# An attention and mixture kernel: output bias as one bf16 pass over three-part factors, a transpose in another PSUM bank, and zeros multiplied before the first data

## The chip, the cores and the metric

The kernel runs on one core of a Trainium2 chip. The metric is the device time of one execution in microseconds (us), the median of several runs. The core has five engines that run their own instruction streams and wait for each other on semaphores: PE (TensorE, matrix multiply), DVE (VectorE), ACT (ScalarE), POOL (GpSimd) and SP (SyncE, which here only issues DMA transfers). PE writes to PSUM, eight banks of 128 partitions by 512 f32.

## What is computed

Input `x` is 8 sequences of 512 rows of 256 numbers. A first layer adds an attention-like gate and normalizes; a second adds a mixture of 12 experts and normalizes again. Cut to what matters here:

```python
x  = layernorm(x + attn(x))                # sum of exp(scores) per row, a small gate, fc2
xa = x @ P_w.T                             # C1, C2, C3: [rows, 12], softmax over the top 3, zero elsewhere
h  = gelu(sum_e C1[:, e:e+1] * (x @ W1[e].T))
y  = sum_e C2[:, e:e+1] * (h @ W2[e].T) + C3 @ b2      # C3 @ b2 is the output bias
x  = layernorm(x + y)
```

## The kernel before, in words

The 4096 rows are 32 tiles of 128 rows (`NT`), in 8 groups of 4 (`GT`, `NG`). The program has two stages.

**The early stage** goes over 8 chunks `c` of attention work: `project(c, 0..3)` on PE (f32, weights `wqk`, input `xTb` from DMA), `qk_copy` on ACT (PSUM bank to SBUF), `rope` on DVE, `scores` on PE, `exps` on ACT, `gate_transpose` on PE. PE, ACT and DVE each begin it with a wait for `ld_const`, six transfers of constants; PE waits for `ld_qk` (`wqk`) too. Beside that the expert weights arrive (`ld_w[0]`, `ld_w[1]`, two transfers of 1 MB and 2 MB each). DVE finds the largest of the first (`w_amax`), ACT sums the second (`w_sum(0)` after chunk 1), and from both come the scales. Then each weight is split into two f16 parts: 8 by ACT and DVE (`w_high`, `w_low`), 16 by POOL (`w_piece`, three instructions each). The group work of the first tiles is placed between chunks by `early_aux`.

**The main stage** is a loop over `i`. In iteration `i`, PE does the second mixture of tile `i-2` (three experts, 18 matmuls with `hT`), transposes the gelu output of tile `i-1` (L916), and does the first mixture of tile `i` (18 matmuls with `x1T`). DVE adds each product with its weight out of PSUM (L1202; of the first mixture ACT takes the first product, L599), ACT does gelu (L604) and the final scaling (L657), POOL the power of the variance (L457 to L459). Products lie in four PSUM banks in turn, so a product waits until the one four places before it has been added. Once in a group of four iterations, with `s = i % 4`, the functions `aux(k, s, pos)` of every engine put in the routing of the next group; `pos` 0 stands ahead of the second mixture, `pos` 1 between the L916 transposes and the first mixture. Order on each engine is the order written in the code.

What the change touches there: at (3, 1) POOL makes the weights of the next group (`weights_of`: L406, L408 for the third weights `C3`, L409 for the others) and then selects those of the chosen experts (`select_of`, six copies at L421). At (0, 0) PE turns `C3`, padded to 32 columns a tile, with one f32 transpose of 128x128 (`C3_transpose`, L772) into `bank[MISC]`, and ACT copies it to `C3T` (L561). At (0, 1) PE computes the router's logits (L755), the gate's `fc` (L732) and, where a group begins, loads the experts' numbers (`load_ids`, L847). At (1, 1) and (2, 1) PE does `bias(g, h)` (L784): one f32 matmul of K = 64 over 512 columns for two tiles; DVE adds it (L1110).

The banks `MISC` (logits, counts, `C3T`), `XPOSE` (the transposes of `x1`, L741, read by ACT's `x1_high` L555 and DVE's `x1_low` L1049) and `ROWS` (`fc` and `bias`) are shared.

## Time and profile before

| | |
|---|---|
| Median of 3 runs | 322.95 us (322.84 to 324.55) |
| Profiled execution, its own time | 323.53 us |
| Its span (first to last instruction) | 321.8 us |
| Granted TensorE clock, mean | 0.981 |
| Busy: PE, DVE, ACT, POOL | 88%, 78%, 48%, 36% |
| Largest groups on PE | L832 mixtures 152.4 us, L688 projections 64.3 us |
| L784 bias matmuls | 32 records, 18.0 us |

How to read it: engines run side by side, so busy shares do not add up, and a group's busy time is not what it costs the kernel. What an edit is worth is read from which wait ends last at its place. Matmul records overlap (their ends are modelled), so the time from one start to the next is the measure of what PE spends. A matmul in f32 leaves two records.

### The profile page before, as it was taken

The page shows a single profiled execution, that of the slowest core. Times are in us where ns is not written, and L with a number is a line of the kernel's source. Part 1 is how long each engine was busy: PE and PEld are TensorE (multiplying, and loading weights), DVE is VectorE, ACT ScalarE, POOL GpSimd, SP SyncE. Part 2 cuts the span into 40 slices and gives each one's busy share as a digit, 9 for nine tenths or more (in the row PEclk, how much of TensorE's full clock was granted, in tenths as well). Part 3 has the DMA queues.
Part 4 walks back from the last instruction along what each step waited for, and adds up shares of the span by engine and source line. Part 5 has one row for each costly group of instructions (what it writes and reads, how often), then busy time and mean ns, then how long its engine had stood idle before and what let it go on. Part 6 is the DMA issues. An engine that isn't in the chain of part 4 may idle for free.

```text
span 321.8 us, 6235 instructions
## 1 busy us (share of the span) xinstructions
PE 282.4 (88%) x1976; PEld 191.8 (60%) x1978; DVE 250.2 (78%) x744; ACT 155.8 (48%) x327; POOL 115.0 (36%) x264
## 2 busy tenths in 40 slices
PE   0999999979784989999999999999999997989981
PEld 0444455444333668677677667677678576667770
DVE  0169789999976579689789879888978977887672
ACT  1138747657561381435635634633733753724331
POOL 1000028999999102142332331522333324132221
PEclk9999999999985999999999999999999999999998
DMA  8999999900000000000010001000100010011011
GB/s 232 415 404 229 200 151 211 144 3 0 0 1 0 3 2 0 18 18 18 18 33 17 18 18 29 22 18 18 34 20 16 18 34 19 18 33 26 26 35 37
DMA packets 19235, 20.58 MB, mean 64 GB/s; under 512 B 1600, under 2 KB 18432, under 8 KB 18688
## 3 DMA queue, kind: packets, MB, share of 16 engines
q1 hardware_dynamic: 18480, 19.22, 24.8%
q10 hardware_dynamic: 720, 0.93, 1.0%
q8 instruction: 18, 0.29, 0.4%
q14 instruction: 17, 0.14, 0.1%
HBM read 15.94 MB, written 4.19 MB: 63 GB/s over the span
## 4 chain that ended last, share of the span: by engine, by line
DVE 25%; PE 21%; issue 6%; ACT 5%; POOL 3%; DVEq 0%; POOLq 0%
PE bank L832 17%; DVE early L1202 11%; DVE st L1239 3%; DVE stats L1038 2%; DVE top L1059 2%; ACT x L548 2%; DVE early L1244 2%; PE bank L784 2%; ACT early L657 1%; POOL rstd L391 1%; PE bank L741 1%; DVE mv L1240 1%; ACT x1T L555 1%; ACT early L604 1%; DVE esum L1104 1%
## 5 line engine op out<-in xcount | busy, mean ns | idle before, releaser
L832 PE MATMUL bank<-W,early 128*128 (+1 forms) x630 | 75.5, 273 | 4.4 <-DVE early L1244 2.3
L832 PE MATMUL bank<-W,x1T 128*128 (+1 forms) x630 | 76.9, 277 | 0.5 <-DVE early L1202 0.3
L832 PEld LDWEIGHTS bank<-W,x1T 128*128 128x128 f16 x630 | 60.3, 99 | 19.8 <-DVE early L1202 9.5
L688 PE MATMUL bank<-early,wqk 128*128 128x512 f32 x128 | 64.3, 634 | 8.5 <-DMA gatew<-in_gate 8.5
L1202 DVE SCALAR_TENSOR_TENSOR early<-bank,Csel,early 128x256 f32<-128x256 f32 x124 | 59.3, 479 | 15.0 <-PE bank L832 10.5
L832 PEld LDWEIGHTS bank<-W,early 128*128 128x128 f16 x630 | 60.1, 98 | 14.8 <-DVE early L1244 3.3
L457 POOL TENSOR_SCALAR ve<-mv 128x1 f32<-128x1 f32 x32 | 7.3, 230 | 117.2 <-DVE mv L1240 117.2
L688 PEld LDWEIGHTS bank<-early,wqk 128*128 128x128 f32 x128 | 23.5, 201 | 30.1 <-issue 20.9
L604 ACT ACTIVATE early<-early 128x256 f32<-128x256 f32 x32 | 13.3, 417 | 48.0 <-DVE early L1202 47.9
L499 ACT ACTIVATE qk<-bank 128x512 bf16<-128x512 f32 x32 | 19.0, 594 | 35.6 <-PE bank L688 35.4
L599 ACT ACTIVATE early<-bank,Csel 128x256 f32<-128x256 f32 x31 | 14.6, 472 | 31.0 <-PE bank L832 30.7
L965 DVE TENSOR_TENSOR xcos<-qk,cb 128x1024 bf16<-128x1024 bf16 x16 | 11.8, 740 | 20.0 <-ACT qk L499 20.0
L390 POOL TENSOR_SCALAR ve<-mv 128x4 f32<-128x4 f32 x8 | 2.3, 283 | 65.1 <-DVE mv L1042 65.0
L647 ACT ACTIVATE early<-bank,ipow 128x256 f16<-128x256 f32 x32 | 15.0, 467 | 16.5 <-PE bank L916 16.5
L382 POOL TENSOR_TENSOR W<-wtmp,W 128x512 f16<-128x512 f32 x16 | 21.1, 1317 | 1.4
L657 ACT ACTIVATE early<-early,shift,rstd 128x256 f32<-128x256 f32 x32 | 18.8, 586 | 5.1 <-POOL shift L459 5.1
L1049 DVE TENSOR_TENSOR x1T<-bank,x1T 128x512 f16<-128x512 f32 x16 | 11.0, 688 | 12.3 <-ACT x1T L555 12.3
L548 ACT ACTIVATE x<-xs,shift,rstd 128x256 f32<-128x256 f32 x32 | 17.4, 591 | 4.3 <-POOL shift L393 4.3
L458 POOL TENSOR_TENSOR rstd<-ve,minus_half 128x1 f32<-128x1 f32 x32 | 18.0, 563 | 2.7
L509 ACT ACTIVATE expd<-bank 128x128 bf16<-128x128 f32 (+3 forms) x32 | 13.7, 435 | 10.0 <-PE bank L703 9.9
L732 PE MATMUL bank<-fc2s,hgT 32*128 32x256 f32 x64 | 18.0, 400 | 0.0
L784 PE MATMUL bank<-b2s,C3T 64*128 64x512 f32 x32 | 18.0, 641 | 0.0
(107 smaller groups left out, 422.3 us busy)
## 6 DMA issues: line engine op xcount, KB each, us to landing
early<-in_xT SPq DMA_DIRECT2D x16, 256.0 KB, 9.8
xs<-in_x SPq DMA_DIRECT2D x32, 128.0 KB, 7.3
out<-early SPq DMA_DIRECT2D x32, 128.0 KB
W<-in_w1T SPq DMA_DIRECT2D x1, 2048.0 KB, 12.0
W<-in_w2T SPq DMA_DIRECT2D x1, 2048.0 KB, 12.3
W<-in_w1T SPq DMA_DIRECT2D x1, 1024.0 KB, 7.6
W<-in_w2T SPq DMA_DIRECT2D x1, 1024.0 KB, 13.8
wqk<-in_wqkT ACTq DMA_DIRECT2D x1, 512.0 KB, 3.8
```

What stands on the lines that cost most here:

```text
L382: pool.tensor_tensor(W[:, m, e + 1, 1, :], wtmp[:, n % 2, :], W[:, m, e + 1, 0, :], ALU.subtract)\
L458: link(pool.tensor_tensor(rstd2[:, p:p + 1], ve2[:, p:p + 1], minus_half[:, 0:1], ALU.pow))
L499: act.activation(qk[:, c % 2, g, :, :].rearrange("p s n -> p (s n)"), bank[PROJ[n % 2]][:, :], ACT.Copy)\
L548: n = act.activation(x1[:, g % 3, t, :], xs[:, GT * g + t, :], ACT.Identity, bias=shift[:, g % 2, t:t + 1], scale=rstd[:, g % 2, t:t + 1])
L604: act.activation(hact[:, t % 2, :], acc1[:, t % 2, :], ACT.Gelu).then_inc(gelu_done, 1)
L647: act.activation(hT[:, t % 2, 0, :, :].rearrange("p c n -> p (c n)"), bank[HT][:, 0:DIM], ACT.Copy, scale=ipow2[:, 1:2]).then_inc(hhi_done, 1)
L657: act.activation(y[:, t % 4, :], y[:, t % 4, :], ACT.Identity, bias=shift2[:, p:p + 1], scale=rstd2[:, p:p + 1]).then_inc(y_done, 1)
L688: mm = pe.matmul(bank[PROJ[n % 2]][:, :], wqk[:, k, g, :], xTb[:, c % 4, k, :, :].rearrange("p s n -> p (s n)"), start=(k == 0), stop=(k = ...
L732: mm = pe.matmul(bank[ROWS][:, t % 2 * DIM:(t % 2 + 1) * DIM], hgT[PAD * T:PAD * (T + 1), u, :, :].rearrange("p b r -> p (b r)"), fc2s[PAD ...
L784: mm = pe.matmul(bank[ROWS][:, :], C3T[rows, :], b2s[rows, :], start=True, stop=True)
L832: mm = pe.matmul(where[:, 0:DIM], lhs(hx, c), w, start=(k == 0), stop=(k == 5))
L1202: dve.scalar_tensor_tensor(sums, bank[place[n]][:, 0:DIM], c, before, ALU.mult, ALU.add)\
```

## The change

1. **The bias in bf16.** `b2` and `C3` are each written as a sum of three bf16 parts. Six products of parts (indices `LEFT` and `RIGHT`) are stacked along K, 6 x 12 = 72 rows, so that one bf16 matmul per tile of K = 72 and 256 columns gives the bias. POOL splits `b2` once at the start (12 partitions, four instructions); SP then spreads the parts to 72 partitions with six transfers in SBUF, in place of four loads from memory.
2. **`C3` is split on POOL** in each group by a new function `C3_split`, four instructions behind `select_of`. `weights_of` now writes `C3f`, and its last instruction waits for that one.
3. **`C3_transpose`** is four bf16 transposes (72 x 128 each) into `bank[XPOSE]` and moves on PE from (0, 0) to (0, 1), ahead of the logits. It no longer waits for `ids_done`; it waits for `x1lo_done`. ACT's `C3T_copy`, now of 72 x 512, moves to (0, 1); in the first group it stands behind `gate_relu(NCH - 1)`.
4. **At the start** PE multiplies zeros (28 matmuls of 256 columns) before it waits for `ld_qk`, and the waits for `ld_const` on PE and ACT move behind the first projections and copies.

```diff
+        WARM = 28
             load_chunk(1)
+            sp.dma_start(b2f[:, :], b2e[1:NS, :]).then_inc(ld_b2, 16)
             load_experts(0, w1T)
...
-            sp.wait_ge(zero_done, 1)
-            for t in range(GT):
-                rows = slice(PAD * t, PAD * (t + 1))
-                sp.dma_start(b2s[rows, t % 2 * DIM:(t % 2 + 1) * DIM], b2e[rows, :]).then_inc(ld_rows, 16)
+            sp.wait_ge(b2_split, 1)
+            for k in range(NP):
+                sp.dma_start(b2s[NE * k:NE * (k + 1), :], b2p[:, RIGHT[k], :]).then_inc(b2_spread, 16)
...
+            pool.wait_ge(ld_b2, 16)
+            link(pool.tensor_copy(b2p[:, 0, :], b2f[:, :]))
+            link(pool.tensor_tensor(b2f[:, :], b2f[:, :], b2p[:, 0, :], ALU.subtract))
+            link(pool.tensor_copy(b2p[:, 1, :], b2f[:, :]))
+            pool.tensor_tensor(b2p[:, 2, :], b2f[:, :], b2p[:, 1, :], ALU.subtract).then_inc(b2_split, 1)
...
             def weights_of(g):
                 pool.wait_ge(recip_done, g + 1)
-                wait(pool, C3T_done, g)
...
-                pool.tensor_tensor(C3[:, :, 1:NS], w[:, :, NM, :], s[:, :, NM, :], ALU.mult).then_inc(C3_done, 1)
+                link(pool.tensor_tensor(C3f[:, :, :], w[:, :, NM, :], s[:, :, NM, :], ALU.mult))
...
+            def C3_split(g):
+                wait(pool, C3T_done, g)
+                f = C3f[:, :, :].unsqueeze(2)
+                link(pool.tensor_copy(C3[:, :, 0:3, :], f.to_broadcast([P, GT, 3, NE])))
+                link(pool.tensor_tensor(C3f[:, :, :], C3f[:, :, :], C3[:, :, 0, :], ALU.subtract))
+                link(pool.tensor_copy(C3[:, :, 3:5, :], f.to_broadcast([P, GT, 2, NE])))
+                pool.tensor_tensor(C3[:, :, 5, :], C3f[:, :, :], C3[:, :, 3, :], ALU.subtract).then_inc(C3_done, 1)
...
                     weights_of(k + 1)
                     select_of(k + 1)
+                    C3_split(k + 1)
...
             def C3_transpose(g):
                 pe.wait_ge(C3_done, g + 1)
-                pe.wait_ge(ids_done, g + 1)
-                pe.transpose(bank[MISC][:, 0:P], C3[:, :, :].rearrange("p t n -> p (t n)"), identf[:, :])\
-                    .then_inc(C3T_done, 1)
+                wait(pe, C3T_copied, g)
+                pe.wait_ge(x1lo_done, min(2 * (g + 2), 2 * NG))
+                spread = bank[XPOSE][0:NP * NE, 0:GT * P // 2].bitcast(BF16)
+                for t in range(GT):
+                    tr = pe.transpose(spread[:, t * P:(t + 1) * P], C3[:, t, :, :].rearrange("p k e -> p (k e)"),
+                                      const(C_IDENT, P))
+                tr.then_inc(C3T_done, 1)
...
-                mm = pe.matmul(bank[ROWS][:, :], C3T[rows, :], b2s[rows, :], start=True, stop=True)
+                if g == 0 and h == 0:
+                    pe.wait_ge(b2_spread, 16 * NP)
+                for t in (2 * h, 2 * h + 1):
+                    mm = pe.matmul(bank[ROWS][:, t % 2 * DIM:(t % 2 + 1) * DIM], C3T[:, t, :], b2s[:, :], start=True, stop=True)
...
             def aux(k, s, pos):
-                if (s, pos) == (0, 0) and group(k):
-                    C3_transpose(k)
                 if (s, pos) == (0, 1):
+                    if group(k):
+                        C3_transpose(k)
                     if group(k + 1):
                         route_logits(k + 1)
...
-            pe.wait_ge(ld_const, 16 * 6)
+            pe.wait_ge(zero_done, 1)
+            for n in range(WARM):
+                pe.matmul(bank[SCORE[n % 2]][:, 0:DIM], zeros[:, 0:P], zeros[:, :], start=True, stop=True)
             pe.wait_ge(ld_qk, 16)
```

How it moves instructions, at the two places of the main loop that matter. First PE, where a group begins (iteration `i = 4k`), before. The names are output `<-` inputs; `C` is the third weights' tile, `early` holds `hT` and the gelu output, and what a row waits for stands in brackets:

```order
L832 MATMUL bank<-W,x1T 128x256 x5
L772 MATMUL bank<-identf,C 128x128 [waits ids_done,C3_done]
L832 MATMUL bank<-W,early 128x256 [waits slot_added,hlo_done]
L832 MATMUL bank<-W,early 128x256 x5
...
L916 MATMUL bank<-identf,early 128x128 [waits hlo_done,gelu_done]
L916 MATMUL bank<-identf,early 128x128
L755 MATMUL bank<-MT,x1T 128x36 [waits C3T_copied,MT_done,x1lo_done]
L755 MATMUL bank<-MT,x1T 128x36 x23
L732 MATMUL bank<-fc2s,hgT 128x256 [waits fc_added]
L732 MATMUL bank<-fc2s,hgT 128x256
L847 TENSOR_LOAD ids [waits ids_done]
```

The same place on PE in the changed kernel, from the L916 transposes on (its lines have other numbers):

```order
L953 MATMUL bank<-identf,early 128x128
L802 MATMUL bank<-cb,C 72x128 [waits x1lo_done,C3T_copied,C3_done]
L802 MATMUL bank<-cb,C 72x128 x3
L782 MATMUL bank<-MT,x1T 128x36 [waits ids_done,MT_done,x1lo_done]
L782 MATMUL bank<-MT,x1T 128x36 x23
L758 MATMUL bank<-fc2s,hgT 128x256 [waits fc_added]
L758 MATMUL bank<-fc2s,hgT 128x256
L880 TENSOR_LOAD ids [waits ids_done]
```

The transpose of the third weights now stands behind the second mixture and the L916 transposes, with its wait for `C3_done`, and ahead of the logits, of `fc` and of the load of the experts' numbers.

Next POOL at the end of a group (`i = 4k + 3`), before:

```order
L459 TENSOR_SCALAR shift<-mv,rstd 128x1 [waits pool_step]
L406 TENSOR_TENSOR escale<-esum,cscale 128x12 [waits C3T_done,recip_done]
L408 TENSOR_TENSOR C<-ez,escale 128x4x12 [waits pool_step]
L409 TENSOR_TENSOR C<-ez,escale 128x8x12
L415 TENSOR_LOAD ids [waits C_done,ids_done]
L421 ISA
L421 COPY Csel<-C 128x4
...
L457 TENSOR_SCALAR ve<-mv 128x1 [waits y_done,mv2_done]
```

And in the changed kernel:

```order
L421 TENSOR_TENSOR escale<-esum,cscale 128x12 [waits recip_done]
L423 TENSOR_TENSOR C3f<-ez,escale 128x48 [waits pool_step]
L424 TENSOR_TENSOR C<-ez,escale 128x8x12 [waits pool_step]
L438 TENSOR_LOAD ids [waits C_done,ids_done]
L444 ISA
L444 COPY Csel<-C 128x4
...
L430 CAST C<-C3f 128x4x36 [waits C3T_done]
L431 TENSOR_TENSOR C3f<-C3f,C 128x48 [waits pool_step]
L432 CAST C<-C3f 128x4x24 [waits pool_step]
L433 TENSOR_TENSOR C<-C3f,C 128x4x12 [waits pool_step]
L482 TENSOR_SCALAR ve<-mv 128x1 [waits y_done,mv2_done]
```

What PE's transpose waits for was L408, the second instruction of `weights_of`. It is now L433, the last of `C3_split`, behind the load, the six copies and three instructions linked one to the next.

## Rows read from the trace of the kernel before

**Rows 1.** Windows, five groups of the main stage, 133.08 to 260.97 us: sums and means
```profile
sum 127.89, PE 120.97 PEld 90.65 DVE 109.77 ACT 65.93 POOL 39.80; mean PE 24.19 PEld 18.13 DVE 21.95 ACT 13.19 POOL 7.96
```

**Rows 2.** Timeline of PE in a group: start, length, line, operation, idle before and releaser
```profile
213.69 2.14 PE L832 MATMUL bank<-W,x1T 128*128 x18
216.13 0.33 PE L772 MATMUL bank<-identf,C 128*128 128x128 f32 x1 [0.30 <-POOL C L408]
...
218.62 0.77 PE L755 MATMUL bank<-MT,x1T 128*128 128x36 f16 x24
...
220.38 2.14 PE L832 MATMUL bank<-W,x1T 128*128 x18
...
224.64 1.12 PE L784 MATMUL bank<-b2s,C3T 64*128 64x512 f32 x2
...
229.47 0.84 PE L832 MATMUL bank<-W,early 128*128 x6 [0.33 <-DVE early L1202]
...
232.15 0.66 PE L741 MATMUL bank<-identf,x 128*128 128x128 f32 x4 [0.31 <-ACT x L548]
```

**Rows 3.** Timeline of DVE in the same group
```profile
215.94 0.48 DVE L1202 SCALAR_TENSOR_TENSOR early<-bank,Csel,early 128x256 f32<-128x256 f32 x1 [0.17 <-PE bank L832]
...
217.88 0.69 DVE L1049 TENSOR_TENSOR x1T<-bank,x1T 128x512 f16<-128x512 f32 x1 [0.86 <-ACT x1T L555]
...
222.77 1.00 DVE L1202 SCALAR_TENSOR_TENSOR early<-bank,Csel,early 128x256 f32<-128x256 f32 x2
```

**Rows 4.** Timeline of POOL in the same group
```profile
216.03 0.35 POOL L409 TENSOR_TENSOR C<-ez,escale 128x96 f32<-128x96 f32 x1
217.21 0.82 POOL L421 COPY Csel<-C 128x4 f32 x6 [0.83 <-POOL C L409]
220.77 0.23 POOL L457 TENSOR_SCALAR ve<-mv 128x1 f32<-128x1 f32 x1 [2.73 <-DVE mv L1240]
221.08 0.56 POOL L458 TENSOR_TENSOR rstd<-ve,minus_half 128x1 f32<-128x1 f32 x1
```

**Rows 5.** Groups by line and form, POOL, five groups of the main stage: busy us, mean ns
```profile
L421 POOL COPY Csel<-C 128x4 f32 x30 | 4.2, 193 | 4.3 <-POOL C L409 4.1 <-issue 0.2
L398 POOL TENSOR_TENSOR ez<-ez,mask 128x144 f32<-128x144 f32 x5 | 2.3, 458 | 0.0
```

**Rows 6.** One line each: duration in ns, shortest, median, longest
```profile
L966 DVE TENSOR_TENSOR xsin<-qk,cb x16: 679/685/1648, 15.6 to 96.6; 128x1024 bf16<-128x1024 bf16 x16
...
L847 PEldq TENSOR_LOAD <-ids x8: 592/680/783, 114.9 to 290.4; - x8
```

**Rows 7.** Timeline of the start, PE, SP and ACT
```profile
8.53 5.71 PE L688 MATMUL bank<-early,wqk 128*128 128x512 f32 x8 [8.53 <-DMA gatew<-in_gate]
...
13.86 0.43 SPq L314 DMA_DIRECT2D W<-in_w2T  x1
...
14.73 7.13 PE L688 MATMUL bank<-early,wqk 128*128 128x512 f32 x16
...
27.27 1.89 ACT L516 ACTIVATE junk<-W 128x2048 bf16<-128x2048 f32 x1
```

**Rows 8.** DMA issues: size, us from issue to landing
```profile
W<-in_w2T SPq DMA_DIRECT2D x1, 2048.0 KB, 12.3
```

**Rows 9.** Timeline at the end of the early stage, PE, and DVE behind it
```profile
101.03 0.45 PE L772 MATMUL bank<-identf,C 128*128 128x128 f32 x1 [5.94 <-DVE ids L1099]
101.27 4.63 PE L832 MATMUL bank<-W,x1T 128*128 128x256 f16 x24
...
118.66 1.01 DVE L1202 SCALAR_TENSOR_TENSOR early<-bank,Csel,early 128x256 f32<-128x256 f32 x2 [1.22 <-ACT early L599]
```

**Rows 10.** The chain that ended last, the last two groups: start, us, what
```profile
275.72 1.05 PE bank L784 x2
276.77 4.04 PE bank L832 x36
...
289.77 0.33 PE bank L772
```

More of the change, by code:

```diff
@@ L35 @@
 WS = NE + 2
+LEFT, RIGHT = (0, 0, 0, 1, 1, 2), (0, 1, 2, 0, 1, 0)
+NP = len(LEFT)
 EPS = 1e-5
@@ L105, in build @@
         fc2s = sb("fc2s", [P, DIM], F32)
-        b2s = sb("b2s", [P, 2 * DIM], F32)
+        zeros = sb("zeros", [P, DIM], BF16)
+        b2f = sb("b2f", [NE, DIM], F32)
+        b2p = sb("b2p", [NE, 3, DIM], BF16)
+        b2s = sb("b2s", [NP * NE, DIM], BF16)
         iota12 = sb("iota12", [P, NE], F32)
@@ L133, in build @@
         Csel = sb("Csel", [P, NT, NM, TOPK], F32)
-        C3 = sb("C3", [P, GT, PAD], F32)
-        C3T = sb("C3T", [P, P], F32)
+        C3f = sb("C3f", [P, GT, NE], F32)
+        C3 = sb("C3", [P, GT, NP, NE], BF16)
+        C3T = sb("C3T", [NP * NE, GT, P], BF16)
         used = sb("used", [1, NM, NE], F32)
@@ L172, in build @@
         ld_rows = sem("ld_rows")
+        ld_b2 = sem("ld_b2")
+        b2_split = sem("b2_split")
+        b2_spread = sem("b2_spread")
         ld_seq = [sem(f"ld_seq{i}") for i in range(4)]
@@ L367, in link @@
                 pool.wait_ge(pool_step, steps[0])
-            pool.memset(b2s[:, :], 0.0).then_inc(zero_done, 1)
+            pool.memset(zeros[:, :], 0.0).then_inc(zero_done, 1)
             pool.memset(ones3[:, :], 1.0).then_inc(zero_done, 1)
             pool.memset(minus_half[:, :], -0.5).then_inc(zero_done, 1)
-            pool.memset(C3[:, :, :], 0.0).then_inc(zero_done, 1)
-            pool.wait_ge(zero_done, 4)
+            pool.wait_ge(zero_done, 3)
+            pool.wait_ge(ld_b2, 16)
[3 more added lines that the diff above has]
+            pool.tensor_tensor(b2p[:, 2, :], b2f[:, :], b2p[:, 1, :], ALU.subtract).then_inc(b2_split, 1)
             def w_piece(n):
@@ L448, in _ @@
             select_of(0)
+            C3_split(0)
             for i in range(NT + 2):
@@ L560, in C3T_copy @@
                 wait(act, bias_done, 2 * g)
-                act.activation(C3T[:, :], bank[MISC][:, 0:P], ACT.Copy).then_inc(C3T_copied, 1)
+                act.activation(C3T[:, :, :].rearrange("p t n -> p (t n)"),
+                               bank[XPOSE][0:NP * NE, 0:GT * P // 2].bitcast(BF16), ACT.Copy).then_inc(C3T_copied, 1)
             def early(k, s, pos):
@@ L576, in aux @@
             def aux(k, s, pos):
-                if (s, pos) == (0, 0):
-                    if group(k + 1):
-                        x1_high(k + 1, 1)
-                    if group(k):
-                        C3T_copy(k)
+                if (s, pos) == (0, 0) and group(k + 1):
+                    x1_high(k + 1, 1)
+                if (s, pos) == (0, 1) and group(k):
+                    C3T_copy(k)
                 if (s, pos) == (1, 0) and group(k + 1):
@@ L604, in gelu @@
                 act.activation(hact[:, t % 2, :], acc1[:, t % 2, :], ACT.Gelu).then_inc(gelu_done, 1)
-            act.wait_ge(ld_const, 16 * 6)
             for c in range(NCH):
@@ L609, in _ @@
                 qk_copy(c, 1)
+                if c == 0:
+                    act.wait_ge(ld_const, 16 * 6)
                 if c:
@@ L631, in _ @@
             aux(0, 0, 0)
-            aux(0, 0, 1)
             begin(0)
@@ L636, in _ @@
             gate_relu(NCH - 1)
+            aux(0, 0, 1)
             gelu(0)
@@ L724, in fc @@
                 if g == 0 and h == 0:
-                    pe.wait_ge(ld_rows, 16 * 5)
+                    pe.wait_ge(ld_rows, 16)
                 if h == 0:
@@ L738, in x1_transpose @@
                 wait(pe, x1lo_done, 2 * g + h)
+                wait(pe, C3T_copied, g - 1)
                 for t in range(2):
@@ L749, in route_logits @@
                     pe.wait_ge(scale_done, 1)
-                wait(pe, C3T_copied, g)
+                wait(pe, ids_done, g)
                 for t in range(GT):
@@ L782, in bias @@
                     wait(pe, bias_added, 2 * g + 1)
-                rows = slice(2 * PAD * h, 2 * PAD * (h + 1))
-                mm = pe.matmul(bank[ROWS][:, :], C3T[rows, :], b2s[rows, :], start=True, stop=True)
+                if g == 0 and h == 0:
+                    pe.wait_ge(b2_spread, 16 * NP)
+                for t in (2 * h, 2 * h + 1):
+                    mm = pe.matmul(bank[ROWS][:, t % 2 * DIM:(t % 2 + 1) * DIM], C3T[:, t, :], b2s[:, :], start=True, stop=True)
                 mm.then_inc(bias_done, 1)
@@ L858, in _ @@
                 if c == 0:
+                    pe.wait_ge(ld_const, 16 * 6)
                     for k in range(NC):
```

## Prediction

> **What bounds the kernel now.** I read the windows of the main stage first, to see whether one engine is full. None is: five middle groups take 127.89 us, 25.58 each, and of that PE is busy 24.19 and DVE 21.95 [rows 1]. What an edit does in one of them counts five times. Then I read the timelines of that group engine by engine, looking only for the idle time ahead of an instruction and for who ended it. PE waits 0.30 us for POOL's third weights, 0.33 for a DVE addition that frees a product bank, and 0.31 for ACT's normalized `x` [rows 2]. DVE waits 0.17 for a product and 0.86 for ACT's copy of `x1T` [rows 3], and the additions at 222.77 wait for nothing. So PE and DVE take turns: PE is the fuller, but after each of its cheap places something else lets it go on. The reader should take from this that PE's time is worth something only where no wait stands behind it. Last I read the chain that ended last. In the two last groups it does run through PE, the bias matmuls included [rows 10]: there no normalization of a coming group is left and PE's time is the kernel's.
>
> **Shorter bias matmuls.** A pass took 1.05 us; 36 matmuls of 256 columns took 4.04, 0.112 each, so two take 0.22 and a pass saves 0.83 [rows 10]. There are 16.
> - In the five middle groups the pass at 224.64 is followed by the wait for DVE at 229.47, the group's second pass by the wait for ACT at 232.15 [rows 2]. Both waits end by work that DVE set in motion, so they grow by what PE saves. I cost the ten passes at nothing; the cover is DVE's own work from 217.88 on. Without that cover they would be worth 8.3 us.
> - Of the first group's two, the first has DVE waiting 1.22 us for ACT beside it [rows 9], so it is hidden; for the second the timeline has no wait close behind, and I count it: -0.8 (bounds 0 and -1.7).
> - The last two groups' four are on the chain: -3.3.
>
> **The transpose of the third weights.** Leaving (0, 0) takes PE's wait of 0.30 and the transpose away at 216.13. It gains nothing by itself: the next product additions start only after DVE's L1049, which waits for ACT [rows 3]. At (0, 1) it waits for the end of `C3_split`. POOL's six copies end at 217.21 + 0.82 = 218.03 [rows 4]; the new link in `weights_of` moves them by 0.1. The four instructions of the split are not in the trace. Two are subtractions of 48 elements; 0.35 for 96 elements and 0.46 for 144 [rows 4, 5] put 48 at 0.25 to 0.28. Two are casts of 144 and 96 elements, between 0.19 (a copy of four elements) and 0.46 (144 elements with two inputs) [rows 5]; with one input I take 0.30 each, nearer the copy. Three links cost 0.08 each (221.00 to 221.08) [rows 4]. Sum 1.4 us, bounds 1.0 (four at 0.19) and 1.7. So PE is released at about 219.55.
>
> The four bf16 transposes: four f32 ones took 0.66 [rows 2], and 4 x 128 columns at the pace above take 0.22. I take 0.25, bounds 0.22 and 0.66. The logits then start at 219.8 where they started at 218.62, 1.2 us late, and so does the first mixture, 220.38 to 221.6 (`fc` and the load of the ids, 0.68 [rows 6], lie between and overlap as before). How much of it DVE feels: in the iteration before, DVE added the third product 2.25 us after the mixture's start (213.69 to 215.94), having waited for it [rows 2, 3]. From 220.38 that is 222.63, but DVE reached it only at 223.27, the second of the two from 222.77 [rows 3]. The slack is 0.64, and 1.2 - 0.64 = 0.56 us is new delay on DVE. All later waits of the group hang on DVE, so the group grows by it: 5 x 0.56 = +2.8. Each 0.1 us of the split, or of the transposes, is 0.5 us here. Behind the waiting transpose stand the logits, `fc`, the ids and the first mixture; who waits for them is DVE (`route_max`, which it reaches well after, so hidden) and DVE and ACT for the products.
>
> In the last two groups PE is the path. Before, PE was released at 289.77 [rows 10] and had about 2.35 us of work up to the first mixture: 18 matmuls at 0.112 and the two L916 transposes. Now it is released 3.4 us after that point, does its transposes (0.25), and in the last group the load of the ids, until now hidden, shows with 0.68 [rows 6], as no `fc` or logits cover it. That is 1.1 us in the one group and 2.1 in the other: +3.2. With the four bias passes the end is -0.1.
>
> ACT's `C3T_copy` grows from 128 to 512 columns; DVE takes 0.69 for 512 [rows 3], I take 0.5 for ACT. In the middle groups it falls into ACT's idle time. In the first it now stands ahead of `gelu(0)`, where DVE waits for ACT [rows 9]: +0.5 (bounds 0.3 and 0.7).
>
> **A rule that speaks against it.** Beside POOL, DVE's L966 has taken up to 1.65 us where the median is 0.69 [rows 6]; but the addition at 215.94 took 0.48 while POOL ran L409 at 216.03 [rows 3, 4], so I add nothing for the additions that will run beside the split. The Trainium skill (Advanced Engine Details and Errata, VectorE Performance Modes) says that VectorE's second port is shared with GpSimd and that the two block each other in the two-port modes. By the rule a DVE instruction in such a mode beside the split would grow as L966 did, by up to 0.96 us a group, 4.8 in five; by the row it is zero, and the row decides.
>
> **The start.** PE's eight first records took 5.71 us, sixteen later ones 7.13, 0.446 each [rows 7]: 2.1 us went to a pace half as fast, the lower of the clock's two levels (1.2 and 2.4 GHz). Zeros multiplied before should take it away, and PE starts before 8.53, as soon as `wqk` and chunk 0 are there. But ACT comes to `w_sum(0)` at 27.27, and that needs the last 2 MB of the second weights, issued at 13.86 and landed 12.3 later, at 26.2 [rows 7, 8]. DMA is full throughout, so this does not come earlier: only 1.1 us of the gain passes, and DVE's scales, POOL's sixteen pieces and all behind them move by that. -1.1 (bounds 0 and -1.3). SP's six small transfers in place of four, and POOL's split of `b2`, are over long before anything needs them.
>
> At the end of the early stage PE stood 5.94 us for `ids_done` and then did four products in 4.63, 0.193 a matmul against the 0.112 of the end, so mostly at the lower clock [rows 9, 10]. Now three of the four can run before; the fourth waits for DVE, which has to finish the ids, `fc_add` and `x1_low` (0.7 each) first. That is worth about 1.7 us at the fourth product. But PE then resumes at the same time as before, with its clock just as low, and the scores and the next products pay for it. I take -0.9 (bounds 0 and -2).
>
> **The sum.** -1.1 - 0.9 + 0.5 - 0.8 + 2.8 - 0.1 = +0.4 against a span of 321.8 us; with 1.7 around it, as in the profiled execution (323.53), 323.9, and against the median of 322.95, **323.3**. From here on I count from the median.
>
> **The rivals.**
> - *The split is slower, or the transposes are* (the other side). Place: PE at (k, 0, 1). Price: with 1.7 for the split and 0.5 for the transposes 0.55 us more in each of seven groups, 327; half of that, 325.3. It decides (past +1.6 us) when split and transposes together exceed 1.9 us where I have 1.65. For it: POOL's casts with a broadcast operand are in no row, and the links may be dearer in four-dimensional forms. Against: no POOL row of this size is over 0.46.
> - *The split is quick and the clock stays up at 101 us.* Split 1.0: -0.4 in each of seven groups, -2.8; 320.5, and with the clock up to 1 us less. For it: copies at 0.19 [rows 5]. Against: 144 elements are not four.
> - *PE is the bound after all.* If DVE had room, a middle group would change by PE's own sum, +1.2 - 1.7 = -0.5, so -2.3 in place of +2.8: 318.2. For it: 24.19 of 25.58 us busy [rows 1]. Against: the two waits behind the two passes [rows 2].
>
> **How the numbers follow.** About 0.5% (1.6 us) is what a measurement of this kernel tells from no change. Forecast, gain and loss about even (321.4 to 324.5): 0.42. Slower split: 0.30. Quick split: 0.20. PE bound: 0.08. So faster 0.28, same 0.42, slower 0.30. The bounds of all terms added up reach from 319 to 329; leaving out PE bound and the last of the slow side, the range is 320.2 to 326.5.
>
> **What would show it.** In the profile after: L714 at 0.43 a record from its first; ACT's `w_sum(0)` at 26.2; the four instructions of `C3_split` with a sum of 1.4 us; PE idle ahead of L802 by about 1 us each group, ended by POOL; the waits behind the two bias passes grown to about 1 us each; a middle group of 26.1 us instead of 25.58; the end shorter by 0.1. Wrong it would be if POOL finished the split before PE arrives at it, if DVE's slack of 0.64 were larger because its own order moved, or if the low clock at 101 us came otherwise.

## The result, and the profile after

The changed kernel takes 335.07 us (median of 4 runs, 334.39 to 335.85) where the kernel before takes 323.13 (4 runs, 322.84 to 324.55): a ratio of 1.036, 95% interval 1.032 to 1.040. It is slower by 12 us. The profiled execution took 334.84 us with a span of 333.1, 11.3 more than before. The times of single executions hang on the granted clock of TensorE, so below I give that clock where they spread.

Page of the changed kernel, the busy times and the clock row (40 slices of the span, tenths of the full clock):

```profile
PE 284.6 (85%) x2028; PEld 201.0 (60%) x2030; DVE 250.0 (75%) x744; ACT 159.0 (48%) x327; POOL 125.0 (38%) x299
...
PEclk9999999999796979979979996999899979997997
```

And the clock row of the page before:

```profile
PEclk9999999999985999999999999999999999999998
```

This is the whole result at a glance. Before, the clock fell twice at the end of the early stage (from 87.6 and from 97.8 us) and never in the main stage but for its last 2 us. After, it falls in those two places again, and then once in nearly every group. The windows of the changed kernel, from the HT transposes of the first group's third tile to the same instruction five groups on, and then each group from one transpose of the third weights to the next (columns: window and length, busy time of each engine with its count, granted clock, DMA share, GB/s):

```profile
133.84:273.20 139.36, 121.74 (x1023) 95.42 (x1021) 110.15 (x386) 68.17 (x130) 45.01 (x150) 0.93 0.07 20
...
142.05:169.67 27.62, 24.05 (x205) 18.81 (x205) 22.03 (x78) 13.61 (x26) 9.00 (x30) 0.94 0.07 21
169.67:197.31 27.64, 24.00 (x205) 18.70 (x205) 22.05 (x78) 13.62 (x26) 9.00 (x30) 0.94 0.07 21
197.31:226.16 28.85, 25.64 (x205) 19.80 (x205) 21.97 (x77) 13.72 (x26) 8.99 (x30) 0.88 0.07 19
```

Five groups took 127.89 before [rows 1] and take 139.36 now. The work of PE became less (the bias passes), yet PE's busy time did not fall with it (121.74 us, before 120.97). One group closer, around the transposes:

```profile
167.70:171.20 3.50, 2.00 (x36) 1.66 (x34) 3.03 (x8) 1.36 (x3) 1.92 (x11) 1.00 0.13 37
171.20:174.60 3.40, 3.40 (x15) 2.02 (x14) 1.66 (x15) 0.47 (x1) 0.82 (x2) 0.50 0.00 0
174.60:198.50 23.90, 20.25 (x191) 16.41 (x189) 20.05 (x62) 13.14 (x25) 7.95 (x27) 1.00 0.09 24
198.50:205.30 6.80, 6.80 (x29) 4.45 (x29) 3.61 (x22) 1.09 (x3) 1.05 (x3) 0.50 0.00 0
```

PE is busy only 2.00 us of the first 3.50, and then works through the next 3.40 at 0.50, the lower level (1.2 GHz). The timeline of PE there, which answers to [rows 2]:

```profile
167.78 0.38 PE L953 MATMUL bank<-identf,early 128*128 128x128 f32 x2
169.67 0.41 PE L802 MATMUL bank<-cb,C 128*72 128x128 bf16 x4 [1.50 <-POOL C L433]
169.92 0.76 PE L782 MATMUL bank<-MT,x1T 128*128 128x36 f16 x24
170.61 1.54 PE L758 MATMUL bank<-fc2s,hgT 32*128 32x256 f32 x4
172.08 3.35 PE L865 MATMUL bank<-W,x1T 128*128 x18
...
181.74 0.84 PE L865 MATMUL bank<-W,early 128*128 x6 [0.60 <-DVE early L1239]
...
182.88 0.38 PE L817 MATMUL bank<-b2s,C3T 72*128 72x256 bf16 x2
184.40 0.66 PE L768 MATMUL bank<-identf,x 128*128 128x128 f32 x4 [1.14 <-ACT x L573]
```

The reader should see three things. PE stands 1.50 us for the end of the split (L433). Right behind it, the mixture that took 2.14 takes 3.35 with the same 18 matmuls. And the waits behind the two shorter bias passes have grown, from 0.33 and 0.31 to 0.60 and 1.14. POOL's split in that group, which answers to [rows 4]:

```profile
168.27 0.30 POOL L430 CAST C<-C3f 128x144 bf16<-128x144 f32 x1
168.65 0.28 POOL L431 TENSOR_TENSOR C3f<-C3f,C 128x48 f32<-128x48 f32 x1
168.99 0.26 POOL L432 CAST C<-C3f 128x96 bf16<-128x96 f32 x1
169.34 0.28 POOL L433 TENSOR_TENSOR C<-C3f,C 128x48 bf16<-128x48 f32 x1
```

168.27 to 169.62 is 1.35 us, where I had 1.4. So the wait itself was foreseen, but not what the clock does behind it. In windows of the granted clock I count eight such dips of about 3.4 us from 119 us to 310 us (one of twice that length counts as two). There is one behind each of the stalls at 142.05, 169.67 and 302.83, two behind 197.31, one behind the 1.14 us waits at 239.26 and 266.93 each, and one behind a wait of 2.25 at 119.21. Waits of the same length also pass with the clock up:

```profile
226.16 0.41 PE L802 MATMUL bank<-cb,C 128*72 128x128 bf16 x4 [1.50 <-POOL C L433]
...
281.40 0.41 PE L802 MATMUL bank<-cb,C 128*72 128x128 bf16 x4 [2.25 <-POOL C L433]
```

So does the stall at 253.83, and so do the waits for `normed` at 156.77, 184.40 and 213.26. A wait of this length can bring a dip; it does not bring one each time.

### The profile page after: what moved, and what is told of

The parts are those of the page before. It is cut to its first block, busy times and chain, and to the rows that moved or that the text cites. A ratio compares the mean times of both kernels' runs of the same rounds, so it can differ in the third digit from the quotient of the medians.

```text
span 333.1 us, 6370 instructions
## 1 busy us (share of the span) xinstructions
PE 284.6 (85%) x2028; PEld 201.0 (60%) x2030; DVE 250.0 (75%) x744; ACT 159.0 (48%) x327; POOL 125.0 (38%) x299
## 4 chain that ended last, share of the span: by engine, by line
PE 36%; POOL 20%; DVE 19%; issue 8%; ACT 6%; SPq 4%; DMA 4%; POOLq 2%; DVEq 0%
PE bank L865 25%; DVE early L1239 7%; POOL W L398 5%; DMA W<-in_w2T 4%; POOL wtmp L395 4%; POOL W L397 3%; PE bank L758 2%; PE bank L714 2%; SPq L325 2%; POOL rstd L407 2%; DVE st L1276 2%; DVE stats L1075 2%; ACT x L573 2%; POOL Csel L444 2%; PE bank L768 1%
## 5 line engine op out<-in xcount | busy, mean ns | idle before, releaser
L865 PE MATMUL bank<-W,x1T 128*128 (+1 forms) x630 | 85.2, 295 | 5.7 <-DVE early L1239 4.1
L865 PE MATMUL bank<-W,early 128*128 (+1 forms) x630 | 78.4, 279 | 6.3 <-DVE early L1281 3.7
L1239 DVE SCALAR_TENSOR_TENSOR early<-bank,Csel,early 128x256 f32<-128x256 f32 x124 | 59.4, 479 | 26.9 <-PE bank L865 21.3
L865 PEld LDWEIGHTS bank<-W,x1T 128*128 128x128 f16 x630 | 64.8, 105 | 23.5 <-DVE early L1239 6.5
L865 PEld LDWEIGHTS bank<-W,early 128*128 128x128 f16 x630 | 61.4, 100 | 18.3 <-issue 4.4
L714 PE MATMUL bank<-early,wqk 128*128 128x512 f32 x128 | 61.7, 613 | 3.5 <-DMA early<-in_xT 1.9
L714 PEld LDWEIGHTS bank<-early,wqk 128*128 128x128 f32 x128 | 22.8, 195 | 24.5 <-issue 22.2
L758 PE MATMUL bank<-fc2s,hgT 32*128 32x256 f32 x64 | 19.3, 422 | 0.0
L768 PE MATMUL bank<-identf,x 128*128 128x128 f32 x64 | 10.9, 296 | 7.9 <-ACT x L573 5.7
```

The source lines that it names most:

```text
L714: mm = pe.matmul(bank[PROJ[n % 2]][:, :], wqk[:, k, g, :], xTb[:, c % 4, k, :, :].rearrange("p s n -> p (s n)"), start=(k == 0), stop=(k = ...
L758: mm = pe.matmul(bank[ROWS][:, t % 2 * DIM:(t % 2 + 1) * DIM], hgT[PAD * T:PAD * (T + 1), u, :, :].rearrange("p b r -> p (b r)"), fc2s[PAD ...
L768: tr = pe.transpose(bank[XPOSE][:, t * DIM + c * P:t * DIM + (c + 1) * P], x1[:, g % 3, 2 * h + t, c * P:(c + 1) * P], identf[:, :])
L865: mm = pe.matmul(where[:, 0:DIM], lhs(hx, c), w, start=(k == 0), stop=(k == 5))
L1239: dve.scalar_tensor_tensor(sums, bank[place[n]][:, 0:DIM], c, before, ALU.mult, ALU.add)\
```

## The experiments

Ratios are to the kernel before, run beside each version (medians 323.96 to 324.04 us).

**Is the idle PE the cause?** PE's idle time ahead of the transposes is filled with work that makes nothing ready sooner.

```diff
             def C3_transpose(g):
-                pe.wait_ge(C3_done, g + 1)
                 wait(pe, C3T_copied, g)
                 pe.wait_ge(x1lo_done, min(2 * (g + 2), 2 * NG))
+                for n in range(12):
+                    pe.matmul(bank[XPOSE][:, 0:DIM], zeros[:, 0:P], zeros[:, :], start=True, stop=True)
+                pe.wait_ge(C3_done, g + 1)
```

> The changed kernel, with 12 matmuls of zeros (256 columns, 1.35 us at 0.112 each) put on PE ahead of its wait for the split third weights, into the bank that the transposes then overwrite. POOL's split and every wait stay as long as they are; PE only does not stand idle in it. Theory A (the idle time of about 1.5 us at this place brings PE's clock down once a group, and that is most of the missing time): the dips of the granted clock in the main stage go away, each of about 3.4 us at half pace worth 1.7 us, seven of them, so 324 to 327 us. Theory B (the clock is not the cause; the delay of the split and of the longer chain through DVE is): 335, since nothing becomes ready sooner. Theory C (the clock falls because the bias passes are shorter, and PE then idles for DVE and ACT behind them): dips stay at about half of the places, 329 to 333.

Measured: 329.42 us (329.32 to 330.0, 4 runs), ratio to before 1.019 (1.015 to 1.022), mean clock 0.974 where the changed kernel had 0.936. Windows by group:

```profile
168.71:195.19 26.48, 23.65 (x219) 19.27 (x217) 22.13 (x77) 13.60 (x26) 9.00 (x30) 1.00 0.08 22
195.19:223.33 28.14, 25.30 (x219) 20.18 (x217) 22.13 (x77) 13.60 (x26) 8.99 (x30) 0.94 0.07 20
```

More work on PE made the kernel 5.6 us faster, so theory B fell. The time lies in theory C's range and above theory A's. The two dips left in the middle groups stand behind ACT's `normed` (L768, 1.14 us). A group with one dip is 28.14 - 26.48 = 1.66 us longer than one without, which is the price of a dip. That it is not 324 to 327 is the edit's own fault. The zeros start only behind the wait for `x1lo_done`, 0.70 us into the stall, and end half a microsecond after the split:

```profile
167.40 1.47 PE L800 MATMUL bank<-zeros 128*128 128x256 bf16 x12 [0.70 <-DVE x1T L1088]
168.71 0.39 PE L804 MATMUL bank<-cb,C 128*72 128x128 bf16 x4
```

**The stall avoided.** The transposes stand behind `route_logits` and `fc` in (0, 1).

```diff
                 if (s, pos) == (0, 1):
-                    if group(k):
-                        C3_transpose(k)
                     if group(k + 1):
                         route_logits(k + 1)
                     if group(k + 2):
                         fc(k + 2, 1)
+                    if group(k):
+                        C3_transpose(k)
```

> The changed kernel, with the transposes of the third weights moved on PE behind the logits and fc of (0, 1), which are 1.9 us of work; the split is then done before PE comes to it, and PE has no stall there. Theory A (the stall of 1.5 us lowers the clock): no dips, and the delay of 1.2 us ahead of the first mixture is gone too: 321 to 324 us. Theory B (only the delay counts, about 0.56 a group and 3.2 in the last two): 335 less 6, 329. Theory C (the waits behind the short bias passes lower the clock): dips stay, behind the waits for ACT's normalized x; 326 to 331.

Measured: 330.89 us median of 8 runs, 325.18 (clock 0.961) to 333.42 (0.937). Its four shortest, up to 330.01, give a ratio of 1.012 (1.007 to 1.017). The only trace is of the longest, 333.42:

```profile
172.02:199.21 27.19, 24.20 (x205) 18.98 (x204) 21.94 (x78) 13.61 (x26) 9.04 (x30) 0.94 0.08 21
...
180.00:183.80 3.80, 2.04 (x16) 1.07 (x14) 3.62 (x15) 2.08 (x6) 1.68 (x4) 1.00 0.02 4
183.80:187.20 3.40, 3.40 (x16) 2.65 (x17) 1.38 (x6) 1.75 (x4) 1.48 (x4) 0.50 0.13 37
```

The stall is gone in the middle groups, and still there is one dip in each of the five, now behind the wait for `normed` (PE busy 2.04 of the 3.80 us ahead of it). Theory A as I put it, that the stall alone does it, is refuted. Theory C holds for this kernel: the dips stand where it says, and its range of 326 to 331 holds the median, though not the executions at 325 and at 333.

**The split cut to one cast.** The second and third parts are left out, so the bias is not the right one.

```diff
             def C3_split(g):
                 wait(pool, C3T_done, g)
                 f = C3f[:, :, :].unsqueeze(2)
-                link(pool.tensor_copy(C3[:, :, 0:3, :], f.to_broadcast([P, GT, 3, NE])))
...
+                pool.tensor_copy(C3[:, :, :, :], f.to_broadcast([P, GT, NP, NE])).then_inc(C3_done, 1)
```

> The changed kernel, but the split of the third weights is a single cast into all six places (the second and third parts are left out, so the bias is not the sum of its parts); the other three instructions and their three links, about 1.1 us, are gone, the order of everything stays. PE's stall should shrink from 1.5 to about 0.5 us. Theory A: dips gone, 322 to 325 us. Theory B: 335 less 0.56 in each of five groups and about 2 at the end, 330. Theory C: dips stay, 328 to 332.

Measured: 324.3 us median of 5 runs, from 320.29 (clock 0.975) to 329.54 (0.944); the three shortest give a ratio of 0.994 (0.987 to 1.000). The windows of the execution of 325.23:

```profile
142.64:168.16 25.52, 22.50 (x204) 18.03 (x205) 21.94 (x78) 13.60 (x26) 8.31 (x27) 1.00 0.08 22
...
193.85:220.71 26.86, 24.02 (x204) 18.99 (x205) 21.88 (x78) 13.60 (x26) 8.30 (x27) 0.94 0.07 20
```

In four of the five middle groups PE's wait at the transposes is 0.70 us now and ends by DVE's L1083, not by the split. In the fifth (193.85) it is 0.86, ended by the cast, and the one dip of the middle groups stands behind that. A group without a dip takes 25.52, 0.06 less than before the change. The waits of 0.60 and 1.14 us behind the bias passes are in all five groups too, and here no dip stands behind them. Between the executions of this one program lie 9 us; their clocks, 0.944 to 0.975, say that the number of dips differs, but only one of them has a trace. Theory A's range holds the median, and no theory foresaw that spread.

**The start alone**, in the kernel before: part 4 of the change and nothing else.

```diff
+            pool.memset(zeros[:, :], 0.0).then_inc(zeros_done, 1)
...
-            pe.wait_ge(ld_const, 16 * 6)
+            pe.wait_ge(zeros_done, 1)
+            for n in range(WARM):
+                pe.matmul(bank[SCORE[n % 2]][:, 0:DIM], zeros[:, 0:P], zeros[:, :], start=True, stop=True)
             pe.wait_ge(ld_qk, 16)
```

> The kernel before, with only part 4 of the change: 28 matmuls of zeros ahead of the wait for wqk, and the waits for the constants behind the first projections and copies. By my prediction this is worth 1.1 us, capped by the landing of the second weights, which ACT's sum waits for: 321.9 us. Rival: the gain of the head is lost in a wait at the end of the early stage, 323; or the later arrival of the x rows in the changed kernel (1 to 4 us later) is due to this part, and it costs time: 324.

Measured: 324.84 us median of 10 runs against 324.04 of 18, ratio 1.001 (0.998 to 1.004). Three executions took 322.6 at a clock of 0.980, seven 324.6 to 325.8 at 0.971 to 0.976. One of the seven, on PE:

```profile
6.99 3.60 PE L693 MATMUL bank<-early,wqk 128*128 128x512 f32 x8
...
29.48 0.70 PE L693 MATMUL bank<-early,wqk 128*128 128x512 f32 x1 [2.84 <-ACT qk L503]
```

The first projections take 3.60 in place of 5.71 [rows 7], as meant. At 29.48 PE then stands 2.84 us for ACT, which waits for the second weights, and the next 3.4 us run at the lower clock. The cap that I had predicted is there, and in this execution it costs: a dip follows the idle time that it makes. 321.9 was expected; the rivals' 323 and 324 are nearer. In the changed kernel PE waits only 1.58 us at this place (28.92), with no dip behind it.

**Which of the two idle times?** The changed kernel with the stall left as it is, and zeros behind the second bias pass.

```diff
             def x1_transpose(g, h):
-                pe.wait_ge(x1_done, 2 * g + h + 1)
                 wait(pe, x1lo_done, 2 * g + h)
                 wait(pe, C3T_copied, g - 1)
+                if g >= 2 and h == 0:
+                    for n in range(8):
+                        pe.matmul(bank[XPOSE][:, 0:DIM], zeros[:, 0:P], zeros[:, :], start=True, stop=True)
+                pe.wait_ge(x1_done, 2 * g + h + 1)
```

> The changed kernel, with 8 matmuls of zeros (256 columns, 0.9 us) on PE behind the second bias pass of a group, where PE otherwise stands 1.14 us for ACT's normalized x. The stall ahead of the split third weights stays. It asks which of two idle times brings the granted clock down. Theory A (the stall ahead of the transposes of the third weights does): dips stay behind that stall once a group, 333 to 335 us. Theory C (the longer wait behind the short bias passes does): dips gone, 326 to 328. Theory D (both places are enough by themselves, whichever of them comes first): dips only behind the stall of the transposes, some fewer than before, 331 to 334.

Measured: 331.11 us (330.18 to 333.68, 4 runs), mean clock 0.950. Windows by group:

```profile
142.25:168.26 26.01, 23.27 (x212) 18.82 (x212) 22.03 (x78) 13.60 (x26) 9.01 (x30) 1.00 0.08 22
168.26:197.12 28.86, 26.57 (x212) 20.45 (x213) 21.98 (x78) 13.74 (x26) 9.00 (x30) 0.88 0.07 20
197.12:223.12 26.00, 23.27 (x213) 18.89 (x213) 22.04 (x78) 13.60 (x26) 9.00 (x30) 1.00 0.08 22
```

The dips that are left stand right behind the stall of 1.5 us, in every other group, twice as long. So theory D is right. With the late transposes only the other wait was left, and here only the stall: each place can bring dips by itself. This run also gives the group with the stall and without a dip: 26.0 us, against 26.1 predicted.

**Both covered**: the late transposes and the 8 zeros together.

> The changed kernel with both idle times taken away: the transposes of the third weights behind the logits and fc, and 8 matmuls of zeros behind the second bias pass. The version with only the first of the two had groups of 27.2 us with one dip each, 25.5 without it. Theories A, C and D all expect the clock up through the middle groups now, groups of 25.5 us, and 324 less up to 2: 321 to 325 us. Theory B, that the clock is only a sign and not the cause, expects 330 as with the transposes moved alone, since zeros make nothing ready sooner.

Measured: 325.26 us median; nine executions lie between 323.14 (clock 0.981) and 325.57 (0.966); ratio 1.003 (1.000 to 1.005), just above the 321 to 325 expected. A tenth execution took 1551.62 us. It is left out of the comparison, and what happened in it stays open. Windows:

```profile
145.03:170.54 25.51, 23.43 (x213) 18.89 (x212) 21.95 (x78) 13.60 (x26) 9.01 (x30) 1.00 0.08 22
170.54:196.05 25.51, 23.43 (x213) 18.75 (x212) 21.95 (x78) 13.60 (x26) 8.99 (x30) 1.00 0.08 22
```

No dip is left in the middle groups, and each takes 25.51. PE multiplies more than in the trace with only the late transposes, and a group is 1.7 us shorter, so theory B is refuted here too. Two dips that the kernel before does not have are left in this trace, one at 120 us and one behind the last group's stall.

**Cheap bias passes alone**, in the kernel before: `C3T` and `b2` in bf16 and one part, nothing moved.

```diff
-        C3T = sb("C3T", [P, P], F32)
+        C3T = sb("C3T", [P, P], BF16)
+        b2h = sb("b2h", [P, 2 * DIM], BF16)
...
-                mm = pe.matmul(bank[ROWS][:, :], C3T[rows, :], b2s[rows, :], start=True, stop=True)
+                mm = pe.matmul(bank[ROWS][:, :], C3T[rows, :], b2h[rows, :], start=True, stop=True)
```

> The kernel before with one edit: the copies of the third weights and of b2 are bf16, one part only (the two lower parts are left out, so the bias has bf16's precision), so that each bias pass is one bf16 matmul of 512 columns, about 0.22 us in place of 1.05. Nothing else moves: no split, no stall. By my prediction's cost of the passes alone: nothing in the middle groups, -0.8 in the first, -3.3 in the last two, 319 us. Theory C (PE's longer waits behind short passes bring the clock down): one dip in most groups, 1.65 each, 322 to 328. Theory A (only the stall of the split does it): 319 to 320, no dips.

Measured: 319.96, 320.11, 327.28 and 327.57 us, at clocks of 0.980, 0.980, 0.961 and 0.966. An execution of the first kind was the profiled one:

```profile
154.29 0.66 PE L745 MATMUL bank<-identf,x 128*128 128x128 f32 x4 [1.04 <-ACT x L552]
...
163.85:189.41 25.56, 22.91 (x199) 17.66 (x200) 21.94 (x78) 13.17 (x26) 7.89 (x27) 1.00 0.08 22
```

The wait grows from 0.31 to 1.04 and takes up what PE saves, so a group stays at 25.56, as I had costed it. With the clock up the whole is worth 4.0 us against the 323.99 of the kernel before beside it (4.1 by the prediction's terms). The other two executions are 3.4 us slower than before. The likely reason is the same dips, as their lower clock says, but neither of them has a trace. So it was tested the other way round, by 7 matmuls of zeros ahead of that wait:

> The kernel before with one-part bf16 bias passes (bf16's precision), and 7 matmuls of zeros (0.8 us) ahead of PE's wait for ACT's normalized x behind the second pass of a group: PE is as busy there as with the f32 passes. The version without the zeros ran 320.0 us in two executions at a mean granted clock of 0.980 and 327.4 in two at 0.961 and 0.966. Theory C (the wait of 1.04 us there tips the clock in some executions): all executions now at about 320 us and 0.98. Rival (the first pass of a group, with its own wait, or another place does it): executions of 323 to 327 us stay.

Measured: 321.66 us (320.76 to 321.95, 4 runs), clock 0.976 to 0.986, ratio 0.993 (0.990 to 0.995). The executions at 327 are gone. With four executions of each, chance is not excluded. Of the 1.6 us against the 320.0 the traces show the place and not the cause: a middle group takes 25.50 (140.16 to 165.66), but the first of them begins at 140.16 in place of 138.26.

**The last group.** Its stall is 2.25 us, and PE sets the end there. Its transposes and ACT's copy move to (1, 0), on top of both covers.

```diff
                 if (s, pos) == (0, 1):
...
-                    if group(k):
+                    if group(k) and k < NG - 1:
                         C3_transpose(k)
+                if (s, pos) == (1, 0) and k == NG - 1:
+                    C3_transpose(k)
```

> As the version with the late transposes and the zeros behind the second bias pass, and in the last group the transposes (and ACT's copy of them) move one iteration on, to (1, 0), where the split is long done. The last group's stall is 2.26 us there, and PE sets the end. Expected by all theories: 1.5 to 2.3 us less than that version, 319 to 323 us, if the last group is bound by PE as the chain shows; nothing, if its end is set by another engine.

Measured: 321.18 us (320.82 to 321.71, 4 runs), ratio 0.991 (0.988 to 0.994). It is the first version with the whole computation that beats the kernel before. It is 4.1 us less than without the edit, where 1.5 to 2.3 were expected: that price left out the dip behind the stall, and 2.25 with 1.65 for the dip would be 3.9. One dip is left in the group before the last, at 271.6 us behind a wait of 1.26 for DVE, and the two next versions have it too.

**The dip at 118 us.** On top of that, 20 matmuls of zeros ahead of the very first bias pass (inside `bias`, where `g == 0 and h == 0`).

> The version with late transposes, zeros behind the second bias pass and the last group's transposes at (1, 0), and 20 more matmuls of zeros (2.2 us) ahead of the very first bias pass, where PE stood 2.83 us for DVE and 6.8 us at the lower clock followed. Theory (any idle time of PE of about a microsecond or more can bring the clock down, and covering it with zeros prevents that): the dip at 118 us goes, 72 products of the second mixture take 8.1 us in place of 10.6, and 1.6 to 3.3 us are won: 318 to 320 us. Rival: DVE sets the time there, and the products only wait less fast: 321, no change. Rival: the clock falls there because of the longer wait at 92 to 101 us, and zeros at 117 come too late: dips stay.

Measured: 320.08 us (318.73 to 321.64, 4 runs), ratio 0.988 (0.983 to 0.992). The windows of the version without these zeros and of this one:

```profile
118.10:124.90 6.80, 5.32 (x26) 3.77 (x27) 5.36 (x19) 3.09 (x5) 1.67 (x4) 0.50 0.00 0
```

```profile
118.00:125.00 7.00, 6.05 (x55) 4.94 (x53) 5.46 (x20) 3.79 (x7) 1.67 (x4) 1.00 0.00 0
```

In about the same stretch PE has 55 instructions in place of 26. The dip there is gone, and with it most of PE's wait (0.64 us in place of 2.83). The median moved by 1.1 us, less than the 1.6 to 3.3 expected, and the runs of the two versions overlap.

**The zeros at the start taken away again** (`WARM = 0`), all else as in the last version.

> The same kernel, but without the 28 matmuls of zeros at the very start (the waits for the constants stay behind the first projections). PE then begins at about 7.6 us at the lower clock, and loses 1.6 us until it rises. By my prediction the head's gain is capped at 1.1 us by the landing of the second weights: 1 us slower than with them. Rival: the gain is lost whole in PE's wait for ACT at about 28 us, and the dip that follows it costs the rest: no slower than with them, or up to 1.6 us faster.

Measured: 320.0 us (319.62 to 320.54, 4 runs), ratio 0.988 (0.986 to 0.990), the same as with them. PE starts at 7.47 at the lower clock and is through the first eight projection records at 12.84, where the changed kernel was at 11.23. But it does not wait at 28 us for ACT any more:

```profile
7.47 5.43 PE L716 MATMUL bank<-early,wqk 128*128 128x512 f32 x8 [7.47 <-DMA early<-in_xT]
...
28.79 1.99 PE L716 MATMUL bank<-early,wqk 128*128 128x512 f32 x4
```

The 28 matmuls at the start are worth nothing in this kernel that these runs can tell; the rival is right.

## Why the prediction was wrong

I forecast 323.3 us (320.2 to 326.5) and 335.07 came. Step by step, with a dip at 1.65 us (1.66 above; 27.62 against the 26.0 of a group with the stall and no dip gives 1.62):

| Stretch of the span | predicted | measured | dips more than before | without them |
|---|---|---|---|---|
| start to the HT transposes at 133.84 (134.54 before) | -2.3 | -0.7 | 1 | -2.35 |
| five groups (139.36, was 127.89) | +2.8 | +11.5 | 6 | +1.6 |
| the rest (59.90, was 59.37) | -0.1 | +0.5 | 1 | -1.15 |
| sum | +0.4 | +11.3 | 8 | -1.9 |

- **The step that failed** is in the part on the shorter bias passes and the transpose: I costed PE's idle time at its delay alone. "I cost the ten passes at nothing", since the waits behind them grow by what PE saves, and the stall at what DVE feels of it. Both costs were right as delays. But the waits of 1.50 and 1.14 us brought the granted clock down, not each time, but with six dips in five groups. The sum has no term for that, and no rival either; I spoke of the clock only at 101 us and at the start, where it was low before. Eight dips are 13.2 us, more than the whole surprise of 10.9.
- **The split**: 1.4 predicted, 1.35 measured. The rival of a slower split is refuted.
- **The transposes**: 0.25 from the first of them to the logits (169.67 to 169.92), as taken.
- **A middle group**: 26.1 predicted, 26.0 measured without a dip. Taken over the five groups the delay was 0.3 to 0.4 each rather than 0.56, so the slack of 0.64 was a little larger than read.
- **The rule on the shared port**: the additions (L1239) beside the split took 484 ns in the median and 486 at most, as before the change. The row gave the right price. The rule of the Trainium skill (Advanced Engine Details and Errata, VectorE Performance Modes) was no real rival for them: the same section asks that source and destination be in SBUF for a two-port mode, and these additions read PSUM. So the 484 ns neither bear it out nor speak against it.
- **The start**: ACT's `w_sum` waits for the second weights as said. The -1.1 for it and the -0.9 for the end of the early stage cannot be told apart in the sum of -2.35. The run without the zeros says that the first is nearer 0; the start alone took 322.6 at a clock of 0.980, 0.4 to 1.1 less than the kernel before at that clock (323.0 to 323.7). At the fourth product the changed kernel is 3.0 us ahead (102.94 against 105.95 at the scores), of which 1.5 is left at the HT transposes (116.36 against 117.87).
- **The last two groups**: -0.1 predicted, -1.1 without the dip. The load of the ids showed with less than I feared: 302.83 to 303.59, 0.76 us from the transposes to the mixture in place of 0.93. And the passes are worth more there: from the L916 transposes to the next mixture it was 1.43 and 1.36 us (275.28 to 276.71, 280.65 to 282.01), and is 0.44 now (286.53 to 286.97), so 0.92 to 0.99 each where I took 0.83.
- **PE bound after all**: refuted. With the clock up and PE lighter (the one-cast and the bf16 runs) a group stays at 25.5.

Why I did not see it: in the trace of before PE's waits in a middle group are 0.42 us and less. Waits as long as the new ones stand only near its end, and the granted clock stays at 1.00 behind them:

```profile
267.28 0.33 PE L772 MATMUL bank<-identf,C 128*128 128x128 f32 x1 [1.46 <-POOL C L408]
...
289.77 0.33 PE L772 MATMUL bank<-identf,C 128*128 128x128 f32 x1 [1.19 <-POOL C L408]
...
312.67 2.14 PE L832 MATMUL bank<-W,early 128*128 x18 [1.48 <-DVE early L1244]
```

By these rows such a wait looks free. They are a few that passed, as some of the changed kernel's do. The trace did show the lower clock behind waits of 2.37 and 5.94 us at the end of the early stage. I read those rows for their pace and not as a warning. The Trainium skill (TensorE: Matmul & The Clock Gate, A second HAM failure mode: psum-queue depth-cycling) tells of a kernel whose clock swings because TensorE idles briefly and often between groups of matmuls. By that rule a loop that gives TensorE new idle times can lose its clock, and the runs here agree: waits of 0.60 to 1.51 us in a loop of 26 us, six dips in five groups. Weighed in the prediction, it would have been the rival on the slow side.

Open: what decides whether a dip follows a wait. Behind the wait of 1.14 us there is one in five of five middle groups with the late transposes, in two of five with the 12 zeros, and in none of five with the one cast. Open too: why the dip behind the stall is sometimes twice as long, and what makes the executions of the one-cast and of the bf16 kernel so different.

## What to carry to other kernels

- Idle time on TensorE has a price of its own besides the delay. Before making its work cheaper, or letting it wait anywhere new, look how long its waits in the loop become. Where they reach a microsecond or more in each turn, as here, add one dip a turn as a rival (here 1.65 us each, in a loop of 26 us). A few such waits in the trace with the clock up do not clear them: the kernel before had three, of 1.19 to 1.48 us.
- If nothing useful can fill such a wait, matmuls of zeros can keep the clock up. Here they cost nothing in the groups where they ended before the wait did (25.51 us a group). Where they outlasted it they cost 0.5 us a group, and where there was no wait, their own time (130.49 to 131.36 with the last group's transposes moved). Put them ahead of all waits of the instruction, and let them end early. Better still, move the waiting instruction behind other work.
- Put a result that takes three or four linked GpSimd instructions where TensorE asks for it last. Here 1.75 us of work (the logits and `fc`) stood ready to cover it.

## What the runs showed of the hardware

- The granted clock fell to its lower level, mostly for 3.4 us, behind one wait of 1.5 us, or behind two of 0.60 and 1.14 us within some 3 us, with TensorE busy on both sides of them. It did not each time: behind the stalls of the changed kernel's five middle groups it did three times of five, and behind waits of 1.46, 1.19 and 1.48 us of the kernel before not at all. One kernel had executions of two kinds, 320.0 and 327.4 us, at clocks of 0.980 and 0.961 to 0.966.
- More matmuls made a kernel faster, twice: 335.07 to 329.42 with 12 zeros a group, and with 8 a kernel of 325.18 to 333.42 came to 323.14 to 325.57 in nine of ten executions, a middle group from 27.2 to 25.5.
- GpSimd: a cast of 144 elements a partition, broadcast threefold on its input, took 0.30 us, one of 96 0.26, a subtraction of 48 elements 0.28, and the link between two of them 0.06 to 0.09.
